# A graph-attention kernel on one core: edge sums as two column tiles of 64, and one-hot product and transpose of a unit next to each other

## The chip, the cores and the metric

The kernel runs on one core of a Trainium2 chip. A core has TensorE (PE in the profile, its weight loads as PEld), VectorE (DVE), ScalarE (ACT), GpSimd (POOL) and SyncE (SP), and 16 DMA engines. The metric is the device time of one execution in microseconds.

## The reference

Two GATv2 attention layers (8 heads, then 4 heads) over 3,125 nodes and 100,000 edges sorted by destination, then a layer norm, then a GIN layer (sum of neighbours and a three-layer MLP) and a second norm. All data is float32. The attention layer, which is what the change touches:

```python
def gatv2_layer(x, src, dst, Wl, Wr, att, bias, n_nodes, heads):
    xl = (x @ Wl).reshape(N, heads, Dh)
    xr = (x @ Wr).reshape(N, heads, Dh)
    e = jax.nn.leaky_relu(xl[src] + xr[dst], NEG_SLOPE)
    logits = jnp.einsum('ehd,hd->eh', e, att)
    m = jax.ops.segment_max(logits, dst, num_segments=n_nodes)
    a = jnp.exp(logits - m[dst])
    denom = jax.ops.segment_sum(a, dst, num_segments=n_nodes)
    alpha = a / denom[dst]
    out = jax.ops.segment_sum(alpha[:, :, None] * xl[src], dst, num_segments=n_nodes)
    return out.mean(axis=1) + bias
...
x = _layernorm(x + _L0_gnn_ref(...))   # two such layers, 8 and 4 heads
x = _layernorm(x + _L1_gnn_ref(...))   # the GIN layer
```

## The kernel before

Edges are cut into units of T = 125 edges that share a window of 32 destination nodes. Twenty units make a chunk (CU = 20), and there are NCH = 45 chunks. `edge_pass` runs once per attention layer: layer 1 has H = 8 heads, C = 4 blocks of 128 columns of the projection and HV = 2 halves of the sums; layer 2 has H = 4, C = 2 and HV = 1.

Each engine walks the chunks in its own program, in NQ = 5 bodies per chunk (q = 0 to 4). A body deals with a group of Q = 4 units. The steps of one group lie in different bodies, which `lag(c, q, n)` says: the group of n bodies ago. TensorE's body, in order, is:

- `turn` (L876 to L892): for the four units of this group, the gathered source rows `xs` (125 edges x 64) are transposed into partitions 0 to 63 of a PSUM bank `ps_x` (L887, float32), and then the destination rows are made by a one-hot product in bf16 into partitions 64 to 127 of the same bank (L890). In the body with q = 0 it first waits for the chunk's gather.
- `project` (L894 to L901), group of one body ago: C products of 128 x 500 in float32 (L900), into two banks `ps_z` in turn; ScalarE's ReLU (L995) empties them, and the wait for it stands ahead of the product two further on.
- `sums` (L943 to L955), group of 15 bodies ago: for each unit and each of the HV halves, a product with the 125 x 128 weights `p` as the stationary and the 65 columns of `xs` as the moving operand (L951), into one of two banks `ps_v`, a pair of units each. VectorE's running add (L1179, L1184 in `run`) empties them; the wait for it stands ahead of every pair.
- `reduce` (L903 to L914), group of 3 bodies ago: eight small products with 32 columns of weights, which go to four column tiles of 32 (L909, L912).
- in q = 0, 1 and 2 a few transposes of the maxima and weights (`maxima_out`, `fifth_out`, `weights_out`: L922, L930, L931, L933, L940), for the chunk before the last.

Before the change a part of `project` and the sums of one unit (layer 1), or of two units (layer 2), take turns, and `reduce` stands ahead of the transposes. GpSimd issues one indirect DMA per unit for the gather (L825; ring `xs` of 6 chunks in layer 1 and 9 in layer 2, freed by the sums' semaphore `v_ready`). VectorE combines the ReLUs (L1090, `combine`), scans for the maxima, weighs (L1162) and adds (`run`) in an order written out by hand; `run` of a group stands in VectorE's body of the same number as its sums on TensorE, with `combine` of another group between the adds. After a layer's chunks the maxima of the last one are stored, and GpSimd gathers them (L831) and the sums (L1271) by node.

A float32 product shows as two MATMUL and two LDWEIGHTS records, a float32 transpose or a bf16 product as one of each; 1800 calls of L909 are 3600 records.

Of the kernel before, what the change touches and what calls it, by code (L numbers as in the profile page):

```python
# [752 lines left out]
def edge_pass(nc, k, lay):  # L753
# [12 lines left out]
    with ExitStack() as ctx:  # L766
# [50 lines left out]
        with nc.Block() as block:  # L817
# [57 lines left out]
            def _(pe):  # L875
                def turn(c, q):  # L876
                    r = c.slot(XR)
                    if q == 0:
                        pe.wait_ge(gath[r], c.uses(XR) * GB)
                        pe.wait_ge(ld_x[c.slot(3)], c.uses(3) * 16 * CU)  # L880
                        pe.wait_ge(s["oht_ready"], c.val(1, 1))
                    if c.after(1) or q >= 2:
                        pe.wait_ge(s["xT_ready"], c.val(NQ, q - 1))
                    ps = ps_x[(c.slot(2) * NQ + q) % 2]
                    for j in range(Q):
                        n = j * NQ + q
                        pe.transpose(ps[0:D, j * T:(j + 1) * T], xs[r][:, n, 0:D], k.ident[0:T, 0:T])  # L887
                    for j in range(Q):
                        n = j * NQ + q
                        ins = pe.matmul(ps[D:128, j * T:(j + 1) * T], xw[c.slot(3)][:, n, :],  # L890
                                        oht[c.slot(2)][:, n * T:(n + 1) * T], start=True, stop=True)
                    ins.then_inc(s["x_ready"], 1)  # L892

                def project(c, q, part):  # L894
                    g = c.slot(XR) * NQ + q
                    if part == 0:
                        pe.wait_ge(s["xT_ready"], c.val(NQ, q + 1))
                    if c.after(1) or C * q + part >= ZR:
                        pe.wait_ge(s["relu_done"], c.val(NQ * C, q * C + part - ZR + 1))
                    pe.matmul(ps_z[part % ZR][:, 0:QT], lay.w_abs[:, part * 128:(part + 1) * 128], xT[q][:],  # L900
                              start=True, stop=True).then_inc(s["z_ready"], 1)  # L901

                def reduce(c, q):  # L903
                    g = c.slot(XR) * NQ + q
                    if c.after(1) or q:
                        pe.wait_ge(s["logit_copied"], c.val(NQ, q))
                    pe.wait_ge(s["combined"], c.val(NQ * (C - 1), (q + 1) * (C - 1)))
                    for j in range(Q):
                        pe.matmul(ps_l[32 * j:32 * j + 32, 0:T], lay.w_lin[:],  # L909
                                  xT[q][:, j * T:(j + 1) * T], start=True, stop=False)  # L910
                    for j in range(Q):
                        ins = pe.matmul(ps_l[32 * j:32 * j + 32, 0:T], lay.sign_sum[:],  # L912
                                        f[g % 3][:, j * T:(j + 1) * T], start=False, stop=True)
                    ins.then_inc(s["logit_ready"], 1)  # L914
# [28 lines left out]
                def sums(c, q, n):  # L943
                    u = Q * q + n
                    st = c.slot(XR) * Q + u // NQ
                    if u % NQ == 0:
                        pe.wait_ge(s["p_ready"], c.val(Q, u // NQ + 1))
                    if n % 2 == 0 and (c.after(1) or u >= 4):
                        pe.wait_ge(s["chain"], c.val(CU, u - 2))
                    for v in range(HV):  # L950
                        ins = pe.matmul(ps_v[u // 2 % 2][:, u % 2 * VX + v * XW:u % 2 * VX + (v + 1) * XW],  # L951
                                        p[st % 3][:, u % NQ, v, :, :].rearrange("e n h -> e (n h)"),
                                        xs[c.slot(XR)][:, u, :], start=True, stop=True)
                    if n % 2:
                        ins.then_inc(s["v_ready"], 2)  # L955

# [2 lines left out]
                def body(c, q):  # L959
                    if c.there():  # L960
                        turn(c, q)
                    zc, zq = lag(c, q, 1)
                    bc, bq = lag(c, q, 15)
                    rc, rq = lag(c, q, 3)
                    for part in range(4):
                        if part % (4 // C) == 0 and (c.after(1) or q >= 1) and zc.there():
                            project(zc, zq, part // (4 // C))
                        if c.after(3) and bc.there():
                            sums(bc, bq, part)
                    if (c.after(1) or q >= 3) and rc.there():  # L970
                        reduce(rc, rq)
                    b = c.back(2)
                    if c.after(2) and b.there():
                        if q == 0:
                            maxima_out(b)
                        if q == 1:
                            fifth_out(b)
                        if q == 2:
                            weights_out(b)
                chunks(pe, LAST, body)  # L980

            @block.scalar
# [1073 lines left out]
```

## Time and profile before

| | |
|---|---|
| median of 3 runs | 4116.12 us (4115.34 to 4116.28) |
| the profiled execution's own time | 4112.72 us |
| its span, first to last instruction | 4110.9 us |
| PE busy | 3302.8 us (80%) |
| POOL / DVE / ACT busy | 2883.6 (70%) / 2788.8 (68%) / 1702.9 us (41%) |
| granted TensorE clock, mean | 0.896 |
| edge pass of layer 1, about | 190 to 1837 us |
| edge pass of layer 2, about | 2104 to 3493 us |

Busy time says for how long an engine had some instruction running. Matmuls overlap, so that PE busy 100% does not mean that the array streams all the time: the gaps between the starts of instructions tell what each one costs. A timeline row gives the start of a group of like instructions in a row, the time until the last of them ended, and how many there are. The start of the next row minus the start of this one is the pace. A PEld row that starts together with its PE row is a weight load that nothing covered; where loads run ahead, the PEld row starts earlier than the PE row.

### The profile page before, as it was taken

The page shows a single profiled execution, that of the slowest core. Times are in us where ns is not written, and L with a number is a line of the kernel's source. Part 1 is how long each engine was busy: PE and PEld are TensorE (multiplying, and loading weights), DVE is VectorE, ACT ScalarE, POOL GpSimd, SP SyncE. Part 2 cuts the span into 40 slices and gives each one's busy share as a digit, 9 for nine tenths or more (in the row PEclk, how much of TensorE's full clock was granted, in tenths as well). Part 3 has the DMA queues.
Part 4 walks back from the last instruction along what each step waited for, and adds up shares of the span by engine and source line. Part 5 has one row for each costly group of instructions (what it writes and reads, how often), then busy time and mean ns, then how long its engine had stood idle before and what let it go on. Part 6 is the DMA issues. An engine that isn't in the chain of part 4 may idle for free. (4 is left out here: it accounts for less than half of the span.)

```text
span 4110.9 us, 76192 instructions
## 1 busy us (share of the span) xinstructions
PE 3302.8 (80%) x24219; PEld 2216.7 (54%) x24219; DVE 2788.8 (68%) x6704; ACT 1702.9 (41%) x3682; POOL 2883.6 (70%) x2229
## 2 busy tenths in 40 slices
PE   0499999999999999986259977777777778457886
PEld 0246666666666666664226645554555546345663
DVE  3558888888888888875527855556555666378872
ACT  3254444444444444412215433333333332156651
POOL 4488888887777777434778888888888883567860
PEclk9999999999999999966679988888888887589897
DMA  2233334343333333222124433333333332112120
GB/s 57 51 67 86 84 83 87 85 87 85 87 84 87 85 85 81 68 59 65 49 42 84 92 67 68 73 67 69 67 72 70 68 68 45 35 34 47 40 46 28
DMA packets 612700, 277.98 MB, mean 68 GB/s; under 512 B 450601, under 2 KB 572877, under 8 KB 611716
## 3 DMA queue, kind: packets, MB, share of 16 engines
q1 hardware_dynamic: 263920, 103.06, 11.5%
q0 software_dynamic: 110784, 80.17, 11.1%
q10 hardware_dynamic: 237600, 89.88, 9.0%
q8 instruction: 198, 3.24, 0.3%
q14 instruction: 198, 1.62, 0.1%
HBM read 164.01 MB, written 106.40 MB: 66 GB/s over the span
## 5 line engine op out<-in xcount | busy, mean ns | idle before, releaser
L900 PE MATMUL L_e_ps_z<-L_e_xT,L_w_abs 128*128 128x500 f32 x2700 | 1496.6, 640 | 0.0
L825 POOL DMA_INDIRECT L_e_xs<-in_x_dram,src_idx x880 | 1185.3, 1347 | 343.9 <-issue 261.0
L825 POOL DMA_INDIRECT L_e_xs<-x_d,src_idx x820 | 1071.2, 1306 | 253.3 <-issue 249.8
L951 PEld LDWEIGHTS L_e_ps_v<-L_e_xs,L_e_p 125*128 125x128 f32 x5400 | 857.2, 203 | 628.1 <-issue 571.6
L995 ACT ACTIVATE L_e_rl<-L_e_ps_z 128x500 f32<-128x500 f32 x1350 | 793.0, 587 | 877.8 <-PE L_e_ps_z L900 877.8
L951 PE MATMUL L_e_ps_v<-L_e_xs,L_e_p 125*128 125x65 f32 x5400 | 793.9, 274 | 12.1 <-DVE L_e_acc L1179 10.4
L1179 DVE SCALAR_TENSOR_TENSOR L_e_acc<-L_e_acc,L_e_row,L_e_ps_v 128x130 f32<-128x130 f32 (+1 forms) x1440 | 448.3, 311 | 426.7 <-PE L_e_ps_v L951 283.1
L887 PE MATMUL L_e_ps_x<-ident,L_e_xs 125*64 125x125 f32 x1800 | 288.1, 285 | 301.5 <-DMA L_e_xs<-x_d,src_idx 245.2
L988 ACT ACTIVATE L_e_xT<-L_e_ps_x 128x500 f32<-128x500 f32 x450 | 264.2, 587 | 610.5 <-PE L_e_ps_x L890 603.8
L900 PEld LDWEIGHTS L_e_ps_z<-L_e_xT,L_w_abs 128*128 128x128 f32 x2700 | 425.7, 197 | 76.2 <-issue 22.4
L1162 DVE TENSOR_TENSOR L_e_p<-L_e_ohc,L_e_ae 125x640 f32<-125x640 f32 x540 | 427.1, 818 | 0.0
L1652 POOL DMA_INDIRECT g_xs<-x_d,src_idx x240 | 295.8, 1233 | 132.9 <-issue 72.5
L887 PEld LDWEIGHTS L_e_ps_x<-ident,L_e_xs 125*64 125x64 f32 x1800 | 188.6, 119 | 345.1 <-DMA L_e_xs<-x_d,src_idx 254.4
L1184 DVE SCALAR_TENSOR_TENSOR L_e_acc<-L_e_acc,L_e_keep,L_e_ps_v 128x65 f32<-128x65 f32 x540 | 134.9, 277 | 304.4 <-PE L_e_ps_v L951 302.3
L1090 DVE SCALAR_TENSOR_TENSOR L_e_f<-L_e_rl,L_sign 128x500 f32<-128x500 f32 x450 | 326.1, 725 | 21.1 <-ACT L_e_rl L995 20.9
L1090 DVE SCALAR_TENSOR_TENSOR L_e_f<-L_e_rl,L_sign,L_e_f 128x500 f32<-128x500 f32 x450 | 330.1, 734 | 4.1 <-ACT L_e_rl L995 0.6
L1768 ACT ACTIVATE g_cnt<-g_ps_c 125x400 bf16<-125x400 f32 x480 | 241.6, 504 | 127.9 <-PE g_ps_c L1703 122.1
L1799 DVE TENSOR_SCALAR g_ohk<-t_keys_n,t_key_of 125x200 bf16<-125x200 bf16 x960 | 225.6, 330 | 7.5 <-PE g_ps_c L1703 7.1
L909 PE MATMUL L_e_ps_l<-L_e_xT,L_w_lin 128*32 128x125 f32 x3600 | 190.3, 283 | 14.1 <-DVE L_e_f L1090 14.1
L1703 PE MATMUL g_ps_c<-g_ohk,g_ohr 125*128 125x200 bf16 x960 | 169.6, 264 | 36.6 <-DVE g_ohk L1799 34.3
L1713 PE MATMUL g_ps_s<-g_x,g_cnt 125*128 125x192 bf16 x1500 | 194.7, 258 | 0.2 <-DVE g_sums L1805 0.2
L890 PE MATMUL L_e_ps_x<-L_e_oht,L_e_xw 96*64 96x125 bf16 x1800 | 192.8, 232 | 0.0
(304 smaller groups left out, 3661.0 us busy)
## 6 DMA issues: line engine op xcount, KB each, us to landing
L_v_d<-L_e_acc ACTq DMA_DIRECT2D x225, 260.0 KB
L_e_dlb<-dloc_d SPq DMA_DIRECT2D x90, 468.8 KB
L_v_d<-L_e_acc ACTq DMA_DIRECT2D x225, 130.0 KB
L_e_xw<-x_d SPq DMA_DIRECT2D x1800, 12.0 KB
L_e_xs<-in_x_dram,src_idx POOLq DMA_INDIRECT x900
L_e_xs<-x_d,src_idx POOLq DMA_INDIRECT x900
L_e_lim<-limits_d SPq DMA_DIRECT2D x180, 39.1 KB
g_xs<-x_d,src_idx POOLq DMA_INDIRECT x240, 3.0
```

Of the source, the lines that this page charges most:

```text
L825: pool.indirect_dma_start(xs[c.slot(XR)][:, n, 0:D], None, lay.x_rows, bass.IndirectOffsetOnAxis(k.src_idx[:, u:u + 1], 0)).then_inc(gath[ ...
L887: pe.transpose(ps[0:D, j * T:(j + 1) * T], xs[r][:, n, 0:D], k.ident[0:T, 0:T])
L900: pe.matmul(ps_z[part % ZR][:, 0:QT], lay.w_abs[:, part * 128:(part + 1) * 128], xT[q][:], start=True, stop=True).then_inc(s["z_ready"], 1)
L951: ins = pe.matmul(ps_v[u // 2 % 2][:, u % 2 * VX + v * XW:u % 2 * VX + (v + 1) * XW], p[st % 3][:, u % NQ, v, :, :].rearrange("e n h -> e ...
L988: act.activation(xT[q][:], ps_x[(c.slot(2) * NQ + q) % 2][:, 0:QT], ACT.Copy).then_inc(s["xT_ready"], 1)
L995: act.activation(rl[n % NE][:], ps_z[part % ZR][:, 0:QT], ACT.Relu, scale=1.0 - SLOPE).then_inc(s["relu_done"], 1)
L1090: dve.scalar_tensor_tensor(out=f[g % 3][:], in0=rl[(C * g + part) % NE][:], scalar=lay.sign[:, part:part + 1], in1=rl[(C * g) % NE][:] if ...
L1162: ins = dve.tensor_tensor(p[n % 3][:, :, v, :, :], ohc[c.slot(2)][:, us, :].unsqueeze(3).to_broadcast([T, NQ, WN, HL]), ae[c.slot(2)][:, u ...
L1179: ins = dve.scalar_tensor_tensor(out=to, in0=prev, scalar=row[c.slot(2)][:, u:u + 1], in1=ps_v[u // 2 % 2][:, u % 2 * VX:(u % 2 + 1) * VX] ...
L1652: pool.indirect_dma_start(xs[p][:, j, :], None, table, bass.IndirectOffsetOnAxis(k.src_idx[:, u:u + 1], 0)).then_inc(gath[p], 16)
L1768: act.activation(cnt[i % CR][:, :, 2 * j:2 * j + 2, :], ps_c[n % 2][0:T, 0:2 * KEYS].rearrange("r (u t n) -> r t u n", u=2, n=EN), ACT.Cop ...
L1799: dve.tensor_scalar(ohk[v % KR][:], keys_n[:], key_of[:, v:v + 1], None, ALU.is_equal).then_inc(s["hot"], 1)
```

## The change

Three edits, all in TensorE's program of `edge_pass`:

1. In `turn` the one-hot product (L890) and the transpose (L887) of a unit now stand next to each other, product first, instead of four transposes and then four products.
2. In `sums` each 128-column product becomes two of 64 columns, whose outputs start at partition 0 and at partition 64.
3. In the body, the sums of all four units stand right behind `turn`, then come all parts of `project`, then the transposes of q = 0, 1, 2, and `reduce` last.

```diff
                     for j in range(Q):
                         n = j * NQ + q
-                        pe.transpose(ps[0:D, j * T:(j + 1) * T], xs[r][:, n, 0:D], k.ident[0:T, 0:T])
-                    for j in range(Q):
-                        n = j * NQ + q
-                        ins = pe.matmul(ps[D:128, j * T:(j + 1) * T], xw[c.slot(3)][:, n, :],
-                                        oht[c.slot(2)][:, n * T:(n + 1) * T], start=True, stop=True)
+                        pe.matmul(ps[D:128, j * T:(j + 1) * T], xw[c.slot(3)][:, n, :],
+                                  oht[c.slot(2)][:, n * T:(n + 1) * T], start=True, stop=True)
+                        ins = pe.transpose(ps[0:D, j * T:(j + 1) * T], xs[r][:, n, 0:D], k.ident[0:T, 0:T])
                     ins.then_inc(s["x_ready"], 1)
...
                     for v in range(HV):
-                        ins = pe.matmul(ps_v[u // 2 % 2][:, u % 2 * VX + v * XW:u % 2 * VX + (v + 1) * XW],
-                                        p[st % 3][:, u % NQ, v, :, :].rearrange("e n h -> e (n h)"),
-                                        xs[c.slot(XR)][:, u, :], start=True, stop=True)
+                        for half in range(2):
+                            ins = pe.matmul(ps_v[u // 2 % 2][64 * half:64 * half + 64, u % 2 * VX + v * XW:u % 2 * VX + (v + 1) * XW],
+                                            p[st % 3][:, u % NQ, v, half * WN // 2:(half + 1) * WN // 2, :].rearrange("e n h -> e (n h)"),
+                                            xs[c.slot(XR)][:, u, :], start=True, stop=True)
...
                     rc, rq = lag(c, q, 3)
-                    for part in range(4):
-                        if part % (4 // C) == 0 and (c.after(1) or q >= 1) and zc.there():
-                            project(zc, zq, part // (4 // C))
-                        if c.after(3) and bc.there():
-                            sums(bc, bq, part)
-                    if (c.after(1) or q >= 3) and rc.there():
-                        reduce(rc, rq)
+                    if c.after(3) and bc.there():
+                        for n in range(Q):
+                            sums(bc, bq, n)
+                    if (c.after(1) or q >= 1) and zc.there():
+                        for part in range(C):
+                            project(zc, zq, part)
                     b = c.back(2)
...
                             weights_out(b)
+                    if (c.after(1) or q >= 3) and rc.there():
+                        reduce(rc, rq)
```

## Rows read from the trace of the kernel before

**Rows 1.** Busy time in two stretches: PE, PEld, DVE, ACT, POOL, granted clock, DMA.

```profile
300.00:1760.00 1460.00, 1460.00 (x10489) 969.84 (x10481) 1217.44 (x2597) 720.80 (x1487) 1095.14 (x811) 1.00 0.38 84
2150.00:3420.00 1270.00, 1027.58 (x8053) 672.38 (x8052) 779.97 (x1873) 485.56 (x1097) 1029.68 (x789) 0.89 0.37 71
```

**Rows 2.** Who waited for whom: us in total, times, longest.

```profile
PE L_e_ps_x L887 <- DMA L_e_xs<-x_d,src_idx: 245.2, 35, 9.5
POOL L_e_xs L825 <- PE L_e_ps_v L951: 62.7, 23, 3.8
```

**Rows 3.** Timeline of PE, one body of layer 1 (q = 4) and the next start.

```profile
916.39 0.62 PE L887 MATMUL L_e_ps_x<-ident,L_e_xs 125*64 125x125 f32 x4
916.94 0.41 PE L890 MATMUL L_e_ps_x<-L_e_oht,L_e_xw 96*64 96x125 bf16 x4
917.28 1.10 PE L900 MATMUL L_e_ps_z<-L_e_xT,L_w_abs 128*128 128x500 f32 x2
918.22 0.56 PE L951 MATMUL L_e_ps_v<-L_e_xs,L_e_p 125*128 125x65 f32 x4
918.62 1.06 PE L900 MATMUL L_e_ps_z<-L_e_xT,L_w_abs 128*128 128x500 f32 x2
919.51 0.56 PE L951 MATMUL L_e_ps_v<-L_e_xs,L_e_p 125*128 125x65 f32 x4
...
922.57 0.42 PE L909 MATMUL L_e_ps_l<-L_e_xT,L_w_lin 128*32 128x125 f32 x8
922.81 0.40 PE L912 MATMUL L_e_ps_l<-L_e_f,L_sign_sum 128*32 128x125 f32 x8
923.13 0.62 PE L887 MATMUL L_e_ps_x<-ident,L_e_xs 125*64 125x125 f32 x4
```

**Rows 4.** Timeline of PEld around another `turn`; in brackets the idle time before.

```profile
1000.65 0.51 PEld L922 LDWEIGHTS L_e_ps_t<-ident,L_e_mx 128*125 128x125 f32 x4 [0.19 <-issue]
1001.08 0.44 PEld L887 LDWEIGHTS L_e_ps_x<-ident,L_e_xs 125*64 125x64 f32 x4
1001.71 0.25 PEld L890 LDWEIGHTS L_e_ps_x<-L_e_oht,L_e_xw 96*64 96x64 bf16 x4 [0.19 <-issue]
```

**Rows 5.** Timeline of PE in the same stretch, and a bf16 product ahead of a float32 one.

```profile
1001.19 0.59 PE L887 MATMUL L_e_ps_x<-ident,L_e_xs 125*64 125x125 f32 x4
...
3679.76 0.36 PE L1703 MATMUL g_ps_c<-g_ohk,g_ohr 125*128 125x200 bf16 x2
3679.96 1.02 PE L1731 MATMUL g_ps_w<-g_blk,g_winhot 96*98 96x512 f32 x2
```

**Rows 6.** Timeline of PE, a body of layer 1 ahead of the first sums.

```profile
229.34 0.62 PE L887 MATMUL L_e_ps_x<-ident,L_e_xs 125*64 125x125 f32 x4
229.88 0.41 PE L890 MATMUL L_e_ps_x<-L_e_oht,L_e_xw 96*64 96x125 bf16 x4
230.22 3.73 PE L900 MATMUL L_e_ps_z<-L_e_xT,L_w_abs 128*128 128x500 f32 x8
233.88 0.42 PE L909 MATMUL L_e_ps_l<-L_e_xT,L_w_lin 128*32 128x125 f32 x8
```

**Rows 7.** Weight loads of eight products in four column tiles of 32.

```profile
3814.64 0.16 PEld L1724 LDWEIGHTS g_ps_p<-g_xs,g_ohn 125*32 125x32 f32 x8
```

**Rows 8.** Timeline of DVE in layer 1: first add of q = 3, last add of q = 4.

```profile
913.42 0.35 DVE L1179 SCALAR_TENSOR_TENSOR L_e_acc<-L_e_acc,L_e_row,L_e_ps_v 128x130 f32<-128x130 f32 x1 [1.75 <-issue]
...
926.05 0.35 DVE L1179 SCALAR_TENSOR_TENSOR L_e_acc<-L_e_acc,L_e_row,L_e_ps_v 128x130 f32<-128x130 f32 x1
```

**Rows 9.** Timelines: last gather and last turn of layer 1, last gather and `L831` of layer 2.

```profile
1696.59 1.21 POOL L825 DMA_INDIRECT L_e_xs<-in_x_dram,src_idx  x1 [0.30 <-issue]
...
1765.75 0.62 PE L887 MATMUL L_e_ps_x<-ident,L_e_xs 125*64 125x125 f32 x4
...
3424.23 1.21 POOL L825 DMA_INDIRECT L_e_xs<-x_d,src_idx  x1 [0.30 <-issue]
3479.15 1.42 POOL L831 DMA_INDIRECT L_node_max<-L_max_d,max_idx  x1 [53.71 <-DMA L_max_d<-L_e_me]
```

## The prediction

> **What bounds the kernel now.** I read the busy time of two long stretches first [rows 1]. In layer 1 (300 to 1760 us) PE is busy 1460 of 1460 us at a granted clock of 1.00, the upper level of 2.4 GHz; VectorE has 1217 and GpSimd 1095. So layer 1 goes at TensorE's pace, and what counts there is the start-to-start time of its instructions. In layer 2 PE has 1028 of 1270 us. The list of waits says what it waits for [rows 2]: 35 waits for the gather, 245 us together, 7.0 us each, one at the head of each chunk. GpSimd issues the gathers of layer 2 with hardly a pause; there a TensorE that is up to 7 us per chunk slower costs nothing. In layer 1 the gathers' queue waited for TensorE only 23 times, 62.7 us in all [rows 2]: so much, and little more, could a faster TensorE win there.
>
> Then the timeline of one body of layer 1 [rows 3]: `turn` 0.89 us (916.39 to 917.28), four times a part of `project` and a unit's sums at 1.29 us (918.22 to 919.51), `reduce` 0.56 us, 6.74 in all. I took the same reading for all five kinds of body: a chunk is 35.39 us (q = 0 to 4: 7.28, 7.40, 7.25, 6.72, 6.74).
>
> **What a switch costs.** The weight loads show it [rows 4]. The load of L890 starts at 1001.71, together with its product and with an idle 0.19 us before it; the load of L887 starts at 1001.08, ahead of its transpose at 1001.19 [rows 5], and with no idle time. So between the transposes (L887) and the one-hot products (L890) the array runs empty, and between L922, which uses all 128 columns, and L887 it does not. Four L887 take 0.55 us to the start of L890 [rows 3]. One is 125 columns in two passes, 250 / 2.4 GHz = 0.104, with 3 ns between instructions 0.107; the first has an uncovered load of 0.03. 0.55 - 4 x 0.107 - 0.03 leaves a gap of 0.095. Four L890 take 0.34: 4 x 0.055 + 0.024 for the first load + 0.095. The same gap stands between L890 and L900, and between L912 (tiles of 32) and L922. It is not the type: a bf16 product goes over to a float32 one at its plain pace (2 x 0.087 of streaming in the 0.20 from 3679.76 to 3679.96) [rows 5]. Nor is it transposing: L922 to L887 has no gap. What is left is the grouping of the columns: L887, though it fills only 64, runs as one array of 128, L890 as a tile of 64, L909 and L912 as tiles of 32, and every change of grouping costs 0.095 us and the cover of the next load.
>
> The Trainium skill (TensorEngine Tiling, Restrictions and Gotchas, Gotcha 2) lists float32 transposes as incompatible with column tiling, and its Key Properties say that a change of tiling mode drains the engine; both speak against edit 1, and by them the sum is the one below.
>
> **Edit 1, turn (layer 1 and 2).** Product and transpose of a unit now alternate between the groupings. A product costs 0.024 + 0.054 + 0.095 = 0.172 to the next start, a transpose 0.028 + 0.105 + 0.095 = 0.228. Four of each: 1.60 us up to the sums. Today 0.89. So +0.71 us a body, before the rest is counted. The lower bound is 0.46 (four transposes that cover the products, no gap); it is rival 2.
>
> **Edit 2, sums.** Today a unit of layer 1 takes 0.40 us from its first record to the next L900 [rows 3], and with the load that L900 then waits for 0.444: four products of 65 columns, paced by loads of 128 columns in two passes (256 / 2.4 = 0.107, seen as 0.111). Four units: 1.78. Afterwards each tile gets 16 products (4 units, 2 halves, 2 records), of 130 / 2.4 = 0.054 streaming and 128 / 2.4 = 0.053 loading. No row shows two tiles of 64. The nearest are the tiles of 32: eight L909 start and end within 0.24 us, where eight in a row would take 0.83 [rows 3], and eight weight loads of L1724, each of about 0.11, lie within 0.16 us [rows 7]. So products and loads of different tiles run at once, and a load under a product of its own tile. I take 0.057 a product: 0.053 (first load) + 16 x 0.057 + 0.095 = 1.06 us. Below, streaming alone gives 1.01; above, tiles whose loads take turns give 16 x 0.111 + 0.15 = 1.93. I stand near the lower end because both rows of narrow tiles do.
>
> **Edit 3, order.** Four parts of `project` back to back exist already, ahead of the first sums [rows 6]: 3.66 us from L900 to L909, a gap and a wait of 0.1 for the third part's bank included (ScalarE's ReLU is not done in time). Today the four parts cost 0.52 + 4 x 0.42 + 3 x 0.47, less than 3.66 by 0.05 only because the sums cover the ReLU. `reduce` stays 0.56, with the gap behind it. The transposes of q = 0 to 2 now follow L900 with no change of grouping: they cost 4 x 0.109 = 0.44 instead of the 0.54 + 0.02 of today [rows 4, 5], and 0.56 instead of 0.69 for q = 1.
>
> The new plain body: 1.60 + 1.06 + 3.66 + 0.56 = 6.88 (today 6.72 and 6.74); q = 0 and 2: 7.32 (7.28, 7.25); q = 1: 7.44 (7.40). A chunk of layer 1: 35.86 instead of 35.39, +0.47. Many gains and losses of 0.7 us cancel here; what is left is 1.3%.
>
> **What waits elsewhere.** VectorE's adds now get all four units at 2.4 us into the body instead of 3.7, and TensorE needs the banks back by 2.1 us into the next one. VectorE's longest stretch is from the first add of q = 3 to the last of q = 4: 913.42 to 926.40, 12.98 us [rows 8]. It would begin at 2.43 of body 3 and end at 15.4; TensorE asks for the bank at 6.88 x 2 + 2.1 = 15.85. It holds by 0.4 us. The gather's wait on `v_ready` moves by less than a body in a ring of six chunks; nothing else is queued behind it. `maxima_out` stands 0.6 us earlier, but its input is ready five microseconds before. ScalarE's copy of `ps_x` and TensorE's next wait for it have a whole body.
>
> **The sum.** Against the profiled execution's own 4112.7 us. 42 chunks of layer 1 have both turns and sums: 42 x 0.47 = +19.7. The bodies ahead of the first sums get +0.71 each; the first ten stand partly behind loads, so I count the last five, +3.6, at most +10.7. At the end of either layer only what leads to the stored maxima counts (L831 and L1271 follow on POOL, and the last sums lie under L831) [rows 9]; there VectorE alternates with TensorE at the lower clock level, where cheaper sums may give back 1 to 5 us in layer 1; I take -3. Layer 2: a body is 1.60 + 0.61 + 1.87 + 0.56 = 4.64 (8 products a tile, two parts of `project`) instead of 4.14, +2.3 a chunk with the transposes. For 44 chunks the gather's 7.0 us hide that; the last has no gather behind it, +2.3, less 0.5. Together 19.7 + 3.6 - 3 + 1.8 = +22, that is 4134.8. The median of the runs shown lies 3.4 us above the profiled execution's own time: 4138 us, +0.5%.
>
> **Rivals.**
> 1. Forecast, as above. With 0.057 to 0.060 a product and 0 to 15 us at the ends: 4128 to 4156 us. Chance 0.68.
> 2. L887 next to L890 does run as a tile of 64. Against it: no gap between L922 and L887 [rows 4]. For it: its output has 64 rows and starts at partition 0, as a tile would. Then `turn` is 0.46 with no gap before the sums, the body 5.74, the chunk 30.1, and the gathers decide instead: their wait of 62.7 us [rows 2] plus the chunk or so (69 us) by which the last gather leads the last turn (1696.6 against 1765.8) [rows 9] allow 63 to 97 us. 4020 to 4053 us. It decides as soon as `turn` falls by more than 0.15 us from today. Chance 0.10. Of the Trainium skill (TensorEngine Tiling, Key Properties) it is the sentence that tiles operate independently that gives this.
> 3. The loads of the two tiles of 64 take turns. For it: today's sums are paced by loads. Against it: the tiles of 32 [rows 3, 7]. Sums 1.93, body 7.75: 210 x 0.87 = +183 us, 4320 us. Chance 0.06. The Trainium skill (TensorE: Matmul & The Clock Gate, Part 3) says that a load overlaps a running product only in another row group, which would give this or worse; the 0.111 us pace of L951, with a load of 0.107 and a product of 0.054, speaks against it.
> 4. The sums, all in one block, meet a bank that VectorE has not emptied. The margin is 0.4 us in q = 0; if VectorE is 0.5 to 1 us later than I count, up to 1 us per chunk: 4145 to 4185 us. Chance 0.08.
> 5. A gap is a little cheaper when groupings alternate at every instruction, or the ends of the layers give back more: 0.02 us off each of eight gaps is 0.16 us a body. Change within 8 us: 4108 to 4124. Chance 0.08.
>
> **How the numbers follow.** A measurement of this kernel tells 0.2%, 8 us, from no change. Slower by more: rivals 3 and 4 and nearly all of the forecast, 0.78. Faster: rival 2 and a little of 5, 0.11. Same: the rest, 0.11. The range leaves out rivals 2 and 3: 4112 to 4180 us.
>
> **What the profile after would show.** L890 and L887 in rows of one, 0.17 and 0.23 us apart, each load with an idle 0.19 or so before it: edit 1. If L887 starts within 0.01 us of L890, it is rival 2. L951 x32 within 0.97 us before the gap: edit 2; 1.8 would be rival 3. L900 x8 3.73 us long: edit 3. A wait of L951 for L1179 or L1184 in q = 0: rival 4. Plain bodies 6.88 us apart in layer 1; in layer 2 the same distance between chunks (30 us) and a shorter wait for the gather, about 4.7 us each. If the layer 2 chunks grow as well, I have the wrong bound there.

## The result and the profile after

The changed kernel takes 4146.8 us (median of 4 runs, 4140.64 to 4154.73) against 4116.1 us for the kernel before on the same chip: a ratio of 1.0076, interval 1.0056 to 1.0096. The forecast was 4138. The profiled execution took 4140.64 us and its span is 4138.8 us, 27.9 more than before.

In the kernel after, L887 is the one-hot product, L889 the transpose, L950 the sums, L898 the projection, L907 and L910 `reduce`. The busy times of the two stretches (columns as in [rows 1]):

```profile
300.00:1760.00 1460.00, 1460.00 (x13562) 796.22 (x13562) 1198.35 (x2556) 695.72 (x1463) 1107.50 (x810) 1.00 0.38 83
2150.00:3420.00 1270.00, 1110.31 (x9616) 624.15 (x9616) 771.71 (x1841) 470.87 (x1091) 1031.58 (x782) 0.90 0.36 71
```

Layer 1 is still at TensorE's pace and at the upper clock level. The other engines' same work is spread over a longer layer: VectorE was busy 1198 us of that stretch instead of 1217. The timeline of PE, one plain body (q = 3), which answers to [rows 3]:

```profile
921.11 0.24 PE L887 MATMUL L_e_ps_x<-L_e_oht,L_e_xw 96*64 96x125 bf16 x1
921.29 0.30 PE L889 MATMUL L_e_ps_x<-ident,L_e_xs 125*64 125x125 f32 x1
921.51 0.24 PE L887 MATMUL L_e_ps_x<-L_e_oht,L_e_xw 96*64 96x125 bf16 x1
921.69 0.30 PE L889 MATMUL L_e_ps_x<-ident,L_e_xs 125*64 125x125 f32 x1
...
922.72 1.15 PE L950 MATMUL L_e_ps_v<-L_e_xs,L_e_p 125*64 125x65 f32 x32
923.80 3.73 PE L898 MATMUL L_e_ps_z<-L_e_xT,L_w_abs 128*128 128x500 f32 x8
927.46 0.42 PE L907 MATMUL L_e_ps_l<-L_e_xT,L_w_lin 128*32 128x125 f32 x8
927.70 0.40 PE L910 MATMUL L_e_ps_l<-L_e_f,L_sign_sum 128*32 128x125 f32 x8
928.02 0.24 PE L887 MATMUL L_e_ps_x<-L_e_oht,L_e_xw 96*64 96x125 bf16 x1
```

The starts give `turn` 1.61 us (forecast 1.60), sums 1.08 (1.06), projection 3.66 (3.66), `reduce` 0.56 (0.56), the body 6.91 (6.88). The product goes to the transpose in 0.18 us, the transpose to the next product in 0.22. From the fourth chunk of layer 1 on, each is the same to 0.01 us: 7.34, 7.47, 7.34, 6.91, 6.91, together 35.97 us, 0.58 more than before.

The waits that answer to [rows 2] (us in total, times, longest):

```profile
PE L_e_ps_x L887 <- DMA L_e_xs<-x_d,src_idx: 165.6, 32, 7.3
POOL L_e_xs L825 <- PE L_e_ps_v L950: 73.5, 28, 3.3
```

Layer 2's wait for the gather is shorter, 5.2 us each time instead of 7.0: TensorE took part of the slack, as forecast. Yet layer 2 became longer. The group of its gathers on GpSimd (busy, mean ns of one | idle before), first of before, then of after:

```profile
L825 POOL DMA_INDIRECT L_e_xs<-x_d,src_idx x820 | 1071.2, 1306 | 253.3 <-issue 249.8 <-POOLq L1488 3.6
```

```profile
L825 POOL DMA_INDIRECT L_e_xs<-x_d,src_idx x820 | 1081.0, 1318 | 253.3 <-issue 249.7 <-POOLq L1488 3.6
```

GpSimd waited for nobody in either; the gather's own operation took 12 ns longer, 9.8 us over 820. The ends of the layers, which answer to [rows 9]:

```profile
1717.85 1.21 POOL L825 DMA_INDIRECT L_e_xs<-in_x_dram,src_idx  x1 [0.30 <-issue]
...
1791.26 0.24 PE L887 MATMUL L_e_ps_x<-L_e_oht,L_e_xw 96*64 96x125 bf16 x1
...
1983.02 2.82 POOL L532 DMA_INDIRECT L_e_xs<-x_d,src_idx  x1 [0.30 <-POOL L_e_xs L632]
...
3451.52 1.21 POOL L825 DMA_INDIRECT L_e_xs<-x_d,src_idx  x1 [0.30 <-issue]
3508.89 1.21 POOL L831 DMA_INDIRECT L_node_max<-L_max_d,max_idx  x1 [56.17 <-DMA L_max_d<-L_e_me]
```

The last turn of layer 1 comes 25.5 us later than before, the first gather of layer 2 (L532; before it stands at 1965.51) 17.5, the last gather of layer 2 27.3, and `L831` of layer 2 29.7. Behind that 1.8 us are given back.

### The profile page after: what moved, and what is told of

Same layout as the page of the kernel before. It is cut to its first block and busy times, and to the rows that moved or that the text cites. A ratio compares the mean times of both kernels' runs of the same rounds, so it can differ in the third digit from the quotient of the medians.

```text
span 4138.8 us, 86902 instructions
## 1 busy us (share of the span) xinstructions
PE 3402.9 (82%) x29619; PEld 1978.9 (48%) x29619; DVE 2793.9 (68%) x6704; ACT 1674.4 (40%) x3682; POOL 2905.0 (70%) x2229
## 5 line engine op out<-in xcount | busy, mean ns | idle before, releaser
L825 POOL DMA_INDIRECT L_e_xs<-in_x_dram,src_idx x880 | 1197.6, 1361 | 353.1 <-issue 259.4
L898 PE MATMUL L_e_ps_z<-L_e_xT,L_w_abs 128*128 128x500 f32 x2700 | 1323.8, 628 | 0.0
L825 POOL DMA_INDIRECT L_e_xs<-x_d,src_idx x820 | 1081.0, 1318 | 253.3 <-issue 249.7
L898 PEld LDWEIGHTS L_e_ps_z<-L_e_xT,L_w_abs 128*128 128x128 f32 x2700 | 457.2, 196 | 524.6 <-ACT L_e_rl L995 267.1
L887 PE MATMUL L_e_ps_x<-L_e_oht,L_e_xw 96*64 96x125 bf16 x1800 | 447.5, 249 | 218.5 <-DMA L_e_xs<-x_d,src_idx 165.6
L889 PE MATMUL L_e_ps_x<-ident,L_e_xs 125*64 125x125 f32 x1800 | 552.6, 307 | 0.0
L950 PE MATMUL L_e_ps_v<-L_e_xs,L_e_p 125*64 125x65 f32 x10800 | 447.8, 234 | 27.9 <-DVE L_e_acc L1179 23.7
L1162 DVE TENSOR_TENSOR L_e_p<-L_e_ohc,L_e_ae 125x640 f32<-125x640 f32 x540 | 427.5, 820 | 0.0
L887 PEld LDWEIGHTS L_e_ps_x<-L_e_oht,L_e_xw 96*64 96x64 bf16 x1800 | 194.2, 108 | 481.6 <-DMA L_e_xs<-x_d,src_idx 174.0
L950 PEld LDWEIGHTS L_e_ps_v<-L_e_xs,L_e_p 125*64 125x64 f32 x10800 | 378.6, 145 | 90.4 <-issue 15.9
L889 PEld LDWEIGHTS L_e_ps_x<-ident,L_e_xs 125*64 125x64 f32 x1800 | 199.9, 111 | 127.4
```

What stands on the lines that cost most here:

```text
L825: pool.indirect_dma_start(xs[c.slot(XR)][:, n, 0:D], None, lay.x_rows, bass.IndirectOffsetOnAxis(k.src_idx[:, u:u + 1], 0)).then_inc(gath[ ...
L889: ins = pe.transpose(ps[0:D, j * T:(j + 1) * T], xs[r][:, n, 0:D], k.ident[0:T, 0:T])
L950: ins = pe.matmul(ps_v[u // 2 % 2][64 * half:64 * half + 64, u % 2 * VX + v * XW:u % 2 * VX + (v + 1) * XW], p[st % 3][:, u % NQ, v, half ...
L1162: ins = dve.tensor_tensor(p[n % 3][:, :, v, :, :], ohc[c.slot(2)][:, us, :].unsqueeze(3).to_broadcast([T, NQ, WN, HL]), ae[c.slot(2)][:, u ...
```

## The experiments

Each ratio is against the kernel before on the same chip. Theories at the start: T, the forecast's own account by changes of grouping; against it VectorE as the next bound, and for layer 2 the question of what sets its length.

### One edit alone, three runs

The kernel before with edit 1 only (`e4_only_turn`):

```diff
-                        pe.transpose(...)      # four, then four products
+                        pe.matmul(...)         # product
+                        pe.transpose(...)      # and transpose of each unit
```

> The kernel before with edit 1 alone: one-hot product and transpose alternate, sums and order as before. Theory: 8 changes of grouping in the turn, turn 1.50 instead of 0.83 us up to the first projection, +0.63 us a body in layer 1, +3.1 us a chunk, 42 chunks +132 us and about +5 at the start; in layer 2 the 7 us wait for the gather hides it: 4240 to 4265 us. Rival (product and transpose run side by side, the loss is elsewhere): faster than before, 4110 us or less.

Measured: 4258.2 us, ratio 1.0335 (1.0314 to 1.0357). Its timeline of PE in layer 1 has the start-to-start times of the kernel after:

```profile
1031.10 0.24 PE L887 MATMUL L_e_ps_x<-L_e_oht,L_e_xw 96*64 96x125 bf16 x1
1031.27 0.30 PE L889 MATMUL L_e_ps_x<-ident,L_e_xs 125*64 125x125 f32 x1
1031.50 0.24 PE L887 MATMUL L_e_ps_x<-L_e_oht,L_e_xw 96*64 96x125 bf16 x1
...
1032.61 1.01 PE L898 MATMUL L_e_ps_z<-L_e_xT,L_w_abs 128*128 128x500 f32 x2
```

The turn is 1.51 us when L898 follows (no change of grouping there). A chunk of layer 1 takes 38.35 us, 2.96 more; 42 of them make 124 us, and by 124 us its last turn is late.

The kernel before with edit 2 only (`e5_only_halves`):

```diff
-                        ins = pe.matmul(ps_v[...][:, ...], p[..., :, :], xs[...])
+                        for half in range(2):
+                            ins = pe.matmul(ps_v[...][64 * half:64 * half + 64, ...], p[..., half * WN // 2:(half + 1) * WN // 2, :], xs[...])
```

> The kernel before with edit 2 alone: sums as two tiles of 64, but still one unit between two parts of the projection. Theory: a unit of layer 1 takes 0.095 (gap) + 0.053 (load) + 4 x 0.057 + 0.095 (gap) + 0.107 (load of the projection, no longer covered) = 0.58 us instead of 0.44, +0.5 us a body, +2.5 a chunk, +105 us: 4205 to 4235 us. Rival (the gap is small between products that are not transposes): sums halve in place, 4080 us or less.

Measured: 4172.0 us, ratio 1.0146 (1.013 to 1.0161), less than expected. In layer 1 a unit's sums and the part of the projection beside them take 1.42 us instead of the 1.29 of [rows 3]:

```profile
1026.88 1.11 PE L900 MATMUL L_e_ps_z<-L_e_xT,L_w_abs 128*128 128x500 f32 x2
1027.92 0.45 PE L952 MATMUL L_e_ps_v<-L_e_xs,L_e_p 125*64 125x65 f32 x8
1028.30 1.10 PE L900 MATMUL L_e_ps_z<-L_e_xT,L_w_abs 128*128 128x500 f32 x2
```

So the halves save 0.02 us of a unit's 0.40 and bring two changes of grouping. The chunk is 37.31 us, 42 x 1.92 = 81 us in all, and the last turn is 81 us late. The rest of the miss lies in layer 2, which became shorter:

```profile
L825 POOL DMA_INDIRECT L_e_xs<-x_d,src_idx x820 | 1055.0, 1287 | 253.2 <-issue 249.7 <-POOLq L1489 3.6
```

The kernel before with edit 3 only (`e6_only_order`), the order of the body as in the kernel after, products of 128 columns:

```diff
-                    for part in range(4):      # a part of project, a unit's sums
-                        ...
+                    for n in range(Q):
+                        sums(bc, bq, n)
+                    for part in range(C):
+                        project(zc, zq, part)
```

> The kernel before with edit 3 alone: all four units' sums (128 columns of weights) in a block, then all projections, transposes, reduce. Theory: the block of sums costs what it did (16 x 0.111 us), the projections get the 0.1 us wait for the ReLU, the transposes of q = 0 to 2 save 0.11 each: +0.1 to +0.3 us a chunk, 4115 to 4130 us, within 0.3% of before. Rival (grouping the sums by itself makes TensorE meet banks that VectorE has not emptied): waits of L951 for VectorE of 0.5 us a chunk or more, 4135 us or more.

Measured: 4137.7 us, ratio 1.006 (1.0047 to 1.0074): a chunk of layer 1 of 35.91 us, 0.52 more. That is above the expected range and inside the rival's, but the rival's cause is not there: the list of waits between 300 and 1760 us has none of L951 for VectorE. A plain body is 6.89 us, by the expectation's own terms 0.89 + 1.78 + 3.66 + 0.56, which it did not add up; the trace has 1.83 for the block of sums and 3.61 for the projection. Alone, edit 3 costs nearly as much as all three together. Together they are no sum (138 + 60 + 26 us against 31), because halves behind one another in one block save what halves in pieces don't.

### One layer alone, two runs

The kernel after, with all three edits in layer 1 only (`e7_layer1_only`) or in layer 2 only (`e8_layer2_only`):

```diff
+                    if not lay.norm:           # layer 1; e8: if lay.norm
+                        ...                    # as after
+                    else:
+                        ...                    # as before
```

> All three edits in layer 1 alone, layer 2 as before. From the traces, layer 1 added 21 us up to the stored maxima, of which 3.5 were given back by the merge: 4133 to 4138 us. If layer 2's 10 us longer gathering came from layer 2's own code (theory A), the gathers of layer 2 take 1459 us again here. If it is chance of the execution or follows from the start time (theory B), they vary between 1459 and 1469 us here as well.

> All three edits in layer 2 alone, layer 1 as before. The prediction's step: the wait for the gather hides all but the last chunk, 4117 to 4120 us. Theory A (layer 2's new order makes the gathers themselves slower, 1.6317 instead of 1.6208 us apart, by more overlap with VectorE's long operations): 4125 to 4135 us, and gathers over 1465 us. Theory B (chance): 4117 to 4120 us.

Measured: 4133.0 us (ratio 1.0047, 1.0033 to 1.0061) and 4124.3 us (1.0031, 1.002 to 1.0043), that is 21.2 and 12.5 us more than before; together 33.6, about the 31 of the whole. The mean gather of layer 2 took 1309 ns in e7 and 1318 in e8, and from first to last the gathers took 1461.1 and 1468.1 us: most of the 10 us comes with layer 2's own order (theory A), though e7 shows 2.4 us without it.

### Why does the kernel not get faster without edit 1? Three misses

The forecast says that edit 1 is the dear one. The kernel after with `turn` as before (`e1_turn_as_before`):

```diff
-                        pe.matmul(ps[D:128, ...], xw[...], oht[...])
-                        ins = pe.transpose(ps[0:D, ...], xs[r][:, n, 0:D], ...)
+                        pe.transpose(ps[0:D, ...], xs[r][:, n, 0:D], ...)   # four
+                        ...
+                        ins = pe.matmul(ps[D:128, ...], xw[...], oht[...])  # then four
```

> The changed kernel with edit 1 undone: four transposes, then four one-hot products; sums in two tiles of 64 and the new order stay. Theory (a change of column grouping costs 0.095 us and the cover of the next load; alternating pays it eight times a body): the turn falls from 1.60 to 0.80 us, because the one-hot products now stand in the same grouping as the sums behind them; a plain body of layer 1 would be 6.1 us and a chunk 31.7 us by TensorE alone. Then the gathers (20 x about 1.64 us = 32.9 us) or VectorE's stretch of 12.98 us set the pace, 32.5 to 33.5 us a chunk: 4005 to 4040 us. Rival (the sums in tiles cost what was lost, not the turn): no faster than before, 4110 us or more.

Measured: 4283.1 us, ratio 1.0394 (1.0374 to 1.0414). A clear miss. The same with a plain float32 product in place of the transpose (`e2_plain_product`), so that it can run as a tile of 64 beside the one-hot product:

```diff
-                        ins = pe.transpose(ps[0:D, ...], xs[r][:, n, 0:D], k.ident[0:T, 0:T])
+                        ins = pe.matmul(ps[0:D, ...], xs[r][:, n, 0:D], k.ident[0:T, 0:T], start=True, stop=True)
```

> The changed kernel with the float32 transpose of the turn replaced by a plain float32 product with the identity matrix (two records instead of one); order and everything else as in the changed kernel. Theory that the gap comes from the grouping, and that only the float32 transpose runs across all 128 columns: the plain product goes to its own tile of 64, starts within 0.01 us of the one-hot product, no idle time between, turn 0.88 to 0.95 us, plain body about 6.2 us, 4015 to 4050 us, although the array streams twice as much for the transposes. Rival (the gap comes from alternating types or kinds of operation, not from the grouping): the gaps stay, turn 1.6 + 0.4 = 2.0 us, body 7.3 us, 4210 us or more.

Measured: 4327.3 us, 1.0508 (1.0482 to 1.0535). The time is a miss, but what the run was built for came true: product and plain product start together, with no gap, and the turn takes 0.70 us.

```profile
1020.75 0.40 PE L910 MATMUL L_e_ps_l<-L_e_f,L_sign_sum 128*32 128x125 f32 x8
1021.08 0.24 PE L887 MATMUL L_e_ps_x<-L_e_oht,L_e_xw 96*64 96x125 bf16 x1
1021.08 0.32 PE L889 MATMUL L_e_ps_x<-ident,L_e_xs 125*64 125x125 f32 x1
...
1021.78 0.27 PE L950 MATMUL L_e_ps_v<-L_e_xs,L_e_p 125*64 125x65 f32 x1
```

So neither the change of type nor the alternation makes the gap, and only the float32 transpose runs across all columns. And with the one-hot products directly ahead of the sums and the transposes behind the sums, ahead of the projection (`e3_three_groupings`):

```diff
                     for n in range(Q):
                         sums(bc, bq, n)
                     ...
+                    turn_rows(c, q)            # the four transposes
```

> As e1, but the four transposes stand behind the sums, next to the projections, so that a body has three changes of grouping (one-hot and sums in 64, then transposes and projections in 128, then reduce in 32) instead of four. Theory: TensorE's own body falls by another 0.10 to 0.13 us against e1. If gathers or VectorE already set the pace in e1, the time is that of e1 within 5 us; if TensorE does, it is 20 to 27 us less than e1.

Measured: 4317.9 us, 1.045 (1.0375 to 1.0525).

The price of the groupings was right: in e1 two of five bodies take 6.05 us, where 6.1 was expected. But a chunk takes 38.9 us on average. Its timeline (L887 transposes, L890 one-hot products, L952 sums, L900 projection), PE, DVE and ACT:

```profile
985.91 0.69 PE L952 MATMUL L_e_ps_v<-L_e_xs,L_e_p 125*64 125x65 f32 x16 [1.04 <-issue]
986.52 3.73 PE L900 MATMUL L_e_ps_z<-L_e_xT,L_w_abs 128*128 128x500 f32 x8
...
991.18 0.62 PE L887 MATMUL L_e_ps_x<-ident,L_e_xs 125*64 125x125 f32 x4
991.73 0.24 PE L890 MATMUL L_e_ps_x<-L_e_oht,L_e_xw 96*64 96x125 bf16 x1
991.74 0.27 PE L952 MATMUL L_e_ps_v<-L_e_xs,L_e_p 125*64 125x65 f32 x1
...
991.98 1.14 PE L952 MATMUL L_e_ps_v<-L_e_xs,L_e_p 125*64 125x65 f32 x29
993.04 1.99 PE L900 MATMUL L_e_ps_z<-L_e_xT,L_w_abs 128*128 128x500 f32 x4
...
995.89 0.35 DVE L1181 SCALAR_TENSOR_TENSOR L_e_acc<-L_e_acc,L_e_row,L_e_ps_v 128x130 f32<-128x130 f32 x1 [3.81 <-remote]
998.13 1.07 ACT L997 ACTIVATE L_e_rl<-L_e_ps_z 128x500 f32<-128x500 f32 x2 [4.74 <-remote]
998.77 3.49 PE L900 MATMUL L_e_ps_z<-L_e_xT,L_w_abs 128*128 128x500 f32 x4 [3.74 <-ACT L_e_rl L997]
```

Read it in order. In q = 0 the second half of the block of sums stops 1.04 us for a bank that VectorE has not emptied (first row; the view names no releaser, but VectorE's add ended 0.06 us before it): rival 4's wait. In the next body the records show the sums done by 993.1 and the first two parts of the projection by 995.0, but VectorE's add starts at 995.89 and ScalarE's ReLU at 998.13, after 3.8 and 4.7 us of idle time. Normally the first ReLU comes 1.1 us after the start of its part. "remote" stands there when the semaphore's update lies at least 1.5 us behind the last record that could have made it. The trace has the times of these updates:

| TensorE's report, e1 | its last record ends | semaphore updated |
|---|---|---|
| sums, first two units | 992.61 | 995.81 |
| sums, last two units | 993.12 | 998.07 |
| projection, part 0 | 994.20 | 998.11 |
| projection, part 1 | 995.03 | 998.15 |

So TensorE's reports came late, and the ring closed: part 3 waits for the late ReLU. The ends of PE's records are modelled, but the updates and the starts of the other engines are not. Two parts whose records end 0.83 us apart report 0.04 us apart, right behind the sums, as if they had been ready and had queued behind them (this is read from the times, not shown). In the whole of layer 1 from 300 to 1700 us, 141 of e1's 345 recorded reports of sums come over 1 us late, in e2 151 of 346 and in e3 122 of 339. Of the 104 bodies of e1 with such a report, 94 are one with a stop in its sums or one of the two behind it. In the kernels before and after, e4, e5 and e6 no report there is over 0.03 us late. The one-hot products fill the upper of the two tiles of 64, and the first sums of the lower tile already run beside them (991.73 and 991.74): the tiles are out of step. Two theories: A, that this is what makes the reports late; B, that the stop does.

### Telling A from B: two runs

The kernel after with the order products, transposes, sums (`e9_product_first`), so that work of the whole array stands between the one tile's products and the sums:

```diff
-                        ins = pe.transpose(...)          # beside each product
+                    for j in range(Q):
+                        n = j * NQ + q
+                        ins = pe.transpose(...)          # four, behind the four products
```

> The kernel after, with the four one-hot products of a body first, then its four transposes, then the sums: between the one-hot products, which run in the upper of the two tiles of 64, and the sums stands work of the whole array. The nothing-else-changed body is 6.04 us (measured in e1_turn_as_before) plus one more change of grouping, 0.095 + 0.05: 6.2 us. Two theories of why e1, e2 and e3 are slow, where TensorE's increments of v_ready come up to 5 us after the last product. A: the sums begin while one-hot products of one tile only still run, so the two tiles are out of step. Then this kernel has none of it: VectorE's longest stretch holds a chunk back by about 1 us, the chunk is 32.5 to 33.5 us, and the gathers' limit of my rival 2 holds, 4015 to 4065 us. B: what matters is that TensorE, in the body of q = 0, stops in the middle of the block of sums for a bank that VectorE has not emptied (1.3 us at 1.15 us into the body in e1), and that the two bodies after it are late. Then this one is late as well, 4200 to 4300 us.

And e1 with its transposes done three times over (`e10_transposes_thrice`), which keeps the tiles out of step but gives VectorE the time:

```diff
-                    for j in range(Q):
+                    for j in [j for _ in range(3) for j in range(Q)]:
                         n = j * NQ + q
                         pe.transpose(...)
```

> e1_turn_as_before with each of the four transposes of a body done three times in a row of blocks of four (the same values written to the same place): eight transposes more, 8 x 0.109 = 0.87 us. The one-hot products still stand directly ahead of the sums, but the plain body is 6.04 + 0.87 = 6.91 us as in the kernel after, so VectorE has emptied the bank in time, as there. Theory A (the tiles out of step): the increments come late as in e1, 4230 us or more. Theory B (the stop inside the block): no late increments, 4130 to 4150 us like the kernel after.

Measured: e9 4073.1 us, ratio 0.9893 (0.9869 to 0.9918), faster than both kernels, 8 us above what A allows and far from B's range; e10 4135.2 us, 1.0069 (1.0052 to 1.0086). e10 has L890 and L952 side by side as e1 has and eight transposes more a body, and its ratio is 0.0325 lower, some 134 us:

```profile
1003.89 1.47 PE L887 MATMUL L_e_ps_x<-ident,L_e_xs 125*64 125x125 f32 x12
1005.29 0.24 PE L890 MATMUL L_e_ps_x<-L_e_oht,L_e_xw 96*64 96x125 bf16 x1
1005.30 0.27 PE L952 MATMUL L_e_ps_v<-L_e_xs,L_e_p 125*64 125x65 f32 x1
...
1005.54 1.10 PE L952 MATMUL L_e_ps_v<-L_e_xs,L_e_p 125*64 125x65 f32 x29
1006.57 3.73 PE L900 MATMUL L_e_ps_z<-L_e_xT,L_w_abs 128*128 128x500 f32 x8
```

No report of e10 in that stretch is over 0.02 us late. So A alone is not enough. But e9 does stop inside the block, once a chunk, and nothing comes late there either (its latest report of layer 1 in that stretch: 0.03 us):

```profile
1001.28 0.69 PE L952 MATMUL L_e_ps_v<-L_e_xs,L_e_p 125*64 125x65 f32 x16
...
1002.72 0.69 PE L952 MATMUL L_e_ps_v<-L_e_xs,L_e_p 125*64 125x65 f32 x16 [0.76 <-DVE L_e_acc L1181]
1003.33 3.73 PE L900 MATMUL L_e_ps_z<-L_e_xT,L_w_abs 128*128 128x500 f32 x8
...
1004.48 0.59 ACT L997 ACTIVATE L_e_rl<-L_e_ps_z 128x500 f32<-128x500 f32 x1 [2.51 <-PE L_e_ps_z L900]
```

The ReLU starts 1.15 us after its part, and the bodies behind the stop take 6.75, 6.63, 6.19 and, without a wait for the gather, 6.19 us. So B alone is not enough either.

Nor is it simply both together. In e1 the first stop inside a block comes at 326.0 us; three bodies before it already report their sums 2.75, 1.84 and 1.67 us late. Two reports of one-hot products come late even ahead of the first sums, 0.46 us at 243.4 and 0.83 us at 268.7, where TensorE's program is that of e6, in which none is late. So the stop is not needed to start the lateness. What is shown is narrower: reports came over 1 us late only in e1, e2 and e3, where the sums stand directly behind products that leave the two tiles out of step, and both additions of whole-array work took it away, the transposes moved between (e9) and eight more transposes ahead (e10). These give time as well as order, and which of the two counts was not tried. What inside TensorE holds the reports back stays open; all executions on record were traced, so that a share of the tracing itself is not excluded.

### What sets layer 2, and a kernel that beats both: two runs

Layer 1 as in e9, layer 2 as before but with edit 2 (`e11_first_and_halves`):

```diff
+                    if not lay.norm:
+                        ...                    # turn of e9, body of after
+                    else:
+                        ...                    # turn and body of before
```

> Layer 1 as in e9_product_first (one-hot products, transposes, sums as two tiles of 64 ahead of the four parts of the projection), which brought layer 2's first gather from 1965.5 to 1897.9 us. Layer 2 with turn and body as before and only its sums as two tiles, as in e5_only_halves, where the 900 gathers of layer 2 took 1288 ns on average and 1442.3 us from first to last, against 1306 ns and 1458.7 before and 1349 ns and 1498.6 in e9. If layer 2 goes by the length of its gathers, and this by the order of the work beside them: 4111 - 68 - 16 = 4027, 4012 to 4045 us. If e9's long gathers in layer 2 came with its early start and not from the order within layer 2: 4055 to 4080 us.

Measured: 4027.8 us, ratio 0.9785 (0.9756 to 0.9814), 2.15% faster than the kernel before. Its first gather of layer 2 starts at 1898.08, and:

```profile
L825 POOL DMA_INDIRECT L_e_xs<-in_x_dram,src_idx x880 | 1222.9, 1390 | 288.2 <-issue 268.0 <-POOLq L605 20.2
L825 POOL DMA_INDIRECT L_e_xs<-x_d,src_idx x820 | 1054.5, 1286 | 253.3 <-issue 249.7 <-POOLq L1521 3.6
```

In layer 1 the gathers now wait for nobody: 20 x (1.39 + 0.30) = 33.8 us is near the mean chunk of 34.0, and GpSimd the new bound. The gathers of layer 2 take 1286 ns as in e5, not the 1354 of e9.

The kernel before, with VectorE's weighted one-hots of layer 2 computed twice (`e12_weigh_twice`):

```diff
+                    if lay.norm:
+                        for v in range(HV):
+                            ins = dve.tensor_tensor(p[n % 3][:, :, v, :, :], ohc..., ae..., ALU.mult)
+                        ins.then_inc(s["again"], 1)
+                        dve.wait_ge(s["again"], c.val(Q, j + 1))
                     for v in range(HV):
```

> The kernel before, with VectorE's weighted one-hots of layer 2 (L1162, 180 operations of 0.82 us) computed twice into the same place; nothing else changed. VectorE has 780 of 1270 us there and takes 148 us more, so it doesn't become the bound. Theory A: what sets layer 2 is the length of the gather's operation on GpSimd, and it grows beside such operations of VectorE. By a fit over the gathers of the profile before, a microsecond of overlap with L1162 lengthens a gather by about 0.5 us; with gathers under way 80% of the time that is 180 x 0.82 x 0.8 x 0.5 = 59 us: 4145 to 4190 us. Theory B: layer 2's time isn't set by that, or the gathers don't mind VectorE: 4105 to 4122 us, mean gather in layer 2 within 10 ns of 1306.

Measured: 4200.8 us, ratio 1.0206 (1.0175 to 1.0236), +85 us, more than the 59 counted and above the range of theory A, far from that of B. VectorE is busy 865 of 1270 us there, so it is not the bound; the gathers are:

```profile
L825 POOL DMA_INDIRECT L_e_xs<-x_d,src_idx x820 | 1154.9, 1408 | 253.4 <-issue 249.8 <-POOLq L1494 3.6
```

102 ns more for each of 820 is 83.7 us, nearly the whole 85. Shown: the length of GpSimd's gather operation sets layer 2, and VectorE's operations lengthen it. The Trainium skill (SBUF — State Buffer, Who interferes with whom) says that a VectorE operation with both inputs in SBUF, as L1162 is, and a GpSimd operation that reads SBUF keep each other off a shared port for as long as the first of them runs; with that rule the runs agree. The same section also tells of a probe in which such an operation did not hold up DMAs; here e12 shows that the gathers' operations get longer. Why the gathers differ between e4, e5, after and e9, where VectorE's operations are the same, would by it be a matter of where they fall; that was not tried by itself, and it is not shown.

| kernel | mean gather of layer 2, ns | first to last gather of layer 2, us |
|---|---|---|
| before, e6 | 1306, 1306 | 1458.7, 1458.5 |
| e7 (layer 2 as before) | 1309 | 1461.1 |
| after, e8 | 1318, 1318 | 1468.5, 1468.1 |
| e4 (edit 1) | 1323 | 1472.8 |
| e5, e11 (edit 2, order before) | 1287, 1286 | 1442.3, 1442.2 |
| e9 | 1354 | 1498.6 |
| e12 | 1408 | 1542.6 |

## Why the prediction was right, and where it was not

**What a switch costs.** Right: 0.18 and 0.22 us to the next start against 0.172 and 0.228, and e4 shows the same alone. The Trainium skill's rule that a change of tiling mode drains the engine (TensorEngine Tiling, Key Properties) agrees, and here the drain costs about 0.1 us and the cover of the next load.

**Edit 2.** Right in size: 1.08 us for the block. Loads of the two tiles run at once, 32 records in 1.08 us. Rival 3 is out. So is the sentence of the Trainium skill (TensorE: Matmul & The Clock Gate, Part 3) that loads overlap running products only in another row group; both tiles use all rows here, and the measurement decides.

**Edit 3.** The projection and `reduce` came out at 3.66 and 0.56. The chunk is 0.11 us over the forecast: 0.02 or 0.03 for each body, from the sums (0.02) and the turn (0.01). Over 42 chunks that is 4.6 us.

**The early bodies.** Forecast +0.71 each, measured +0.52, since L898 follows the last transpose without a change of grouping (turn 1.51) and the projection took 3.56 us there; the prediction's step forgot that there are no sums in between. At 285 us the kernel is 1.4 us late instead of 3.6.

**The end of layer 1.** Forecast -3; from the last turn (+25.5) to the first gather of layer 2 (+17.5) 8 us are given back. Of these 4.4 lie ahead of `L831` and 3.6 in the merge behind it. This term was too small.

**Layer 2.** The step that failed: "for 44 chunks the gather's 7.0 us hide that", +1.8. TensorE's extra time was hidden, the wait fell from 7.0 to 5.2 us; but the gathers themselves took 9.8 us more, and the last gather leads `L831` by 57.4 us instead of 54.9. e8 shows this layer's +12.5 alone. The prediction took the bound's own operation for fixed. e12 shows that it is not.

So (19.7 + 3.6) - 3 + 1.8 = 22 was in truth 25.5 (chunks and early bodies, to the last turn of layer 1) - 8.0 (end of layer 1) + 9.8 (gathers of layer 2) + 2.4 (its end) - 1.8 (behind it) = 27.9, and misses of opposite sign hid each other in part. The other 3 us lie between the profiled execution (4140.6) and the median (4146.8): 6.2 where 3.4 were added.

**Rivals.** 1 came true. 2 is out: L887, now L889, has a gap on both sides. 3 is out by the 1.08 us of the block. 4 did not come in the kernel after: no wait of TensorE for a bank in layer 1 between 300 and 1750 us. But its price was near: e9, whose bodies are 0.7 us shorter, stops about 1 us per chunk, as the margin says: TensorE comes back two bodies later, 2 x 0.7 us sooner, less 0.4. 5 is out: the gaps did not get cheaper (0.18 and 0.22 us), and the change is 31 us. What the prediction did not have is that TensorE's reports can come late. In e1 that makes a chunk 38.9 us, in e9, with bodies 0.15 us longer, 34.0; the expectations of e1, e2 and e3 fell on that.

## What to carry to other kernels

Count changes of column grouping in TensorE's program as instructions of about 0.1 us, and order the work so that neighbours share one: four products, four transposes and then the sums (e9) take 0.89 us where the pairs take 1.61. Work of the whole array between products of a single tile and a block that uses several tiles paid here (e9 against e1), though why is open. When an engine idles and the trace names no releaser, look at when its semaphore was updated, not only at the records that should have done it. And where an engine's own operation is the bound, as GpSimd's gathers are here, look at what runs beside it: an edit of TensorE's program that is hidden behind the gathers can still move VectorE's work against them.

## What the runs showed of the hardware

- A float32 transpose of 64 output columns runs in the grouping of the whole array: a gap of about 0.1 us on either side next to tiles of 64, none next to products of 128 columns (turn 1.61 us ahead of the sums, 1.51 ahead of L898). A plain float32 product in its place runs as a tile of 64, beside the bf16 product in the other tile (both start at 1021.08 in e2).
- Two tiles of 64: 32 records of 65 columns in float32, each with its own load, start to next L898 in 1.08 us.
- TensorE's reports of finished work came up to 5 us after its records' ends in e1 (sums of 993.12 reported at 998.07), also ahead of any stop (2.75 us late at 299.9), and within 0.03 us in the kernel after. Then engines stand still for which the view names no releaser ("remote"), and the records of TensorE look done.
- The gather's operation on GpSimd took 1286 to 1408 ns on average in the same layer with the same indices, as the order of the other engines' work changed; 148 us more of one VectorE operation lengthened 820 gathers by 84 us (e12).
